# Joining the head of a vision-transformer kernel into one embedding loop, moving the zero stores to the sync engine, and reordering the first expert loads

## The chip, the cores and the metric

The kernel runs on one core of a Trainium2 chip. The metric is device time in microseconds (us), the median of three runs. The core has a matrix engine (PE, TensorE; its weight loads are listed as PEld), a vector engine (DVE), an activation engine (ACT), GpSimd (POOL), and a sync engine (SP), which here issues most of the DMAs. "SPq", "ACTq" and "PEq" in a profile are those engines' sequencers at work on register, wait and DMA-issue instructions.

## The reference

Input x is 32 images of 3 x 96 x 96. All values are float32.

```
h  = patches(x) @ W.T + b                      # 32 images x 36 tokens x 192
xm, ref = h[:22], h[22:]                       # 10 reference images
e(z) = gelu(z @ fc1 + b1) @ fc2 + b2           # 192 -> 48 -> 24, for own and reference tokens
mask = 0.5 + 0.5 * tanh(12.5 * mean over refs of cosine(e(xm), e(ref)))
k    = ref @ k_w ;  q, v = split(x @ qv_w)
three times, from x = xm * mask:
    a = q k^T * scale ; a = a a^T ; o = mean over refs of a v
    x = layernorm(o @ proj + b)
...                                            # combined with h, layernorm
x = x + softmax attention(layernorm(x))        # 12 heads, 36 tokens per image
x = x + mixture of 8 experts, top 2 (192 -> 768 -> 192)
out = layernorm(h + x)
```

Because `a a^T` only needs the product of the reference keys with themselves, the kernel forms one Gram matrix k^T k per pair of heads over all reference tokens and folds it into the query weights once.

## The kernel before

**Tiles.** The 1152 tokens are cut into NT = 11 tiles of T = 108 (three images); the last tile has 72. MT = 8 tiles hold tokens of the 22 own images; tile 7 holds own and reference images, and tiles 7 to 10 hold the references. The work is written out by hand per engine: each engine has a program of its own, and semaphores (`S["h_ready"]` and so on) order them. Nothing is scheduled by a planner.

**Head, in phases.** SP (L301 to L311) issues the loads: `tokw`, token tiles 0 and 1, the eleven small tensors of `EARLY`, token tiles 2 to 10, then `DIFF` and `FFN`. PE (L399 to L414) makes one token product per tile (L408, six matmuls of 192 columns, each recorded as two) into PSUM bank 0 or 1 and transposes the previous tile (L414). DVE adds the bias (L953), after a wait on all of `EARLY` (L950), and PE waits on the same set before tile 1 (L402). ACT copies each transpose to `hT` (L734). Then come, one after the other: the fc1 products in three chunks (L419), gelu (L737), four key products for tiles 7 to 10 (L425), eleven fc2 products (L429), the Gram matrices (L437), the folded weights `wqg` (L442), the sum of the reference embeddings `rb` (L449), and on DVE the squares and norms (L956 to L969), cosines (L973, L974), tanh on ACT (L754), the mask (L976 to L979) and the masked tiles `xs` (L981). The first transpose of the diffusion loop (L462) waits for `xs` of tile 0.

**Zeros.** The buffer `srt_dram`, into which the token rows are later scattered by expert, must hold zeros first. ACT issues nine stores for this (L740 to L742, 7.15 MB by the page's queue q10), placed between the gelus and the evictions of the key products (L743 to L750), so these evictions stand behind the nine issues in ACT's program.

**Middle.** Diffusion (NI = 24 turns of a software-pipelined loop, L468), then attention with the second layernorm, gate logits, top 2 and destination computation (L553). In both PE is the engine with the most work. In diffusion SP also stages the expert weights, ACT and POOL split them into two 16-bit parts.

**Experts.** POOL scatters the rows of each tile by two indirect DMAs (L1245). DVE computes which expert each of the NTILE = 25 tiles of 128 sorted rows belongs to (L1113 to L1130, `exp_ready`) and where its rows start (L1133, `place_ready`). SP waits for `exp_ready` (L359), issues the weights of the first WB = 3 tiles (L360, L349, two DMAs of 384 KB each), waits for `place_ready` and for all 22 scatters (L362, L363), and then loads the rows of the first tiles (L364, L356). PE transposes the rows of tile i+1 (L655) before the products of tile i. ACT, DVE and POOL scale and split the transposed rows, and PE does the expert's two layers (L669 to L671, L684 to L686). From the fourth tile on SP alternates rows and weights.

**End.** The results are scattered to `y_dram`, read back, summed and normalised.

## Time and profile before

| what | us |
|---|---|
| median of 3 runs (463.40 to 466.49) | 465.44 |
| the profiled execution's own time | 462.96 |
| its span, first to last instruction | 461.1 |
| first diffusion transpose starts | 65.36 |
| rows of the first expert tile arrive | 334.27 |

| engine | busy us | share of the span |
|---|---|---|
| PE | 370.7 | 80% |
| DVE | 249.3 | 54% |
| POOL | 213.8 | 46% |
| ACT | 202.5 | 44% |

How to read it: busy time is averaged over stages with different limits. The profiled execution took 1.9 us more than its span. The page's 40 slices (11.5 us each) show PE nearly full in most of them and nearly empty in the fifth (46 to 58 us), in those around 185 to 207 us, and around 320 to 334 us. The chain that ended last lists, from first to last instruction, the work or wait that each next step stood on; a piece on it has nothing beside it that ended later.

### The profile page before, as it was taken

How to read it: one execution, taken by the hardware profiler on the slowest of the kernel's cores; microseconds unless marked ns; L12 is line 12 of the kernel's file. 1: busy time of each engine (PE TensorE's matmuls, PEld its weight loads, DVE VectorE, ACT ScalarE, POOL GpSimd, SP SyncE). 2: the span in 40 equal slices, each digit the busy share in tenths (PEclk: the TensorE clock that was granted, in tenths of full speed). 3: DMA queues.
4: the chain of work that ended last, by engine and by line, in shares of the span. 5: the costliest groups of instructions: out<-in, count | busy, mean ns of one | idle time of the engine just before them, and what ended most of it. 6: DMA issues, size and time to landing. Idle time of an engine off the chain costs nothing.

```text
span 461.1 us, 10989 instructions
## 1 busy us (share of the span) xinstructions
PE 370.7 (80%) x3682; PEld 316.6 (69%) x3682; DVE 249.3 (54%) x713; ACT 202.5 (44%) x507; POOL 213.8 (46%) x355
## 2 busy tenths in 40 slices
PE   3998258999999974307999999974089999999964
PEld 3995245667667653206889999974079989999963
DVE  2111043445545476642467776756448888888723
ACT  1113313677777754213366567431054554444303
POOL 1000000276766655861256776545125666676424
PEclk9899559999999997555899999985569999999989
DMA  8905932665666653000000000013537767667042
GB/s 254 359 2 169 335 118 63 178 137 147 148 137 146 136 138 88 0 1 1 1 2 13 19 18 28 17 31 97 224 108 254 254 244 255 247 246 258 19 146 86
DMA packets 59558, 59.08 MB, mean 128 GB/s; under 512 B 36939, under 2 KB 46197, under 8 KB 58736
## 3 DMA queue, kind: packets, MB, share of 16 engines
q1 hardware_dynamic: 56240, 47.66, 34.2%
q10 hardware_dynamic: 1008, 7.15, 4.7%
q0 software_dynamic: 2256, 3.57, 2.5%
q8 instruction: 32, 0.52, 0.5%
q14 instruction: 22, 0.18, 0.1%
HBM read 25.11 MB, written 14.33 MB: 86 GB/s over the span
## 4 chain that ended last, share of the span: by engine, by line
PE 68%; DVE 8%; issue 7%; ACT 5%; POOL 4%; ACTq 3%; SPq 2%; DMA 2%; POOLq 0%; DVEq 0%
PE bank L385 37%; PE wide L385 26%; ACTq L741 3%; PE bank L390 3%; ACT xT L860 2%; DVE xs L1007 1%; PE bank L655 1%; POOL rstd L1212 1%; DMA bdm<-in_bdm 1%; SPq L349 1%; PE bank L569 1%; SPq L305 1%; ACT xTs L759 1%; DVE xT L1022 1%; ACT xs L777 1%
## 5 line engine op out<-in xcount | busy, mean ns | idle before, releaser
L1240 POOL TENSOR_TENSOR w1l<-xT,w1h 128x768 bf16<-128x768 f32 x8 | 13.2, 1644 | 81.1 <-ACT w1h L726 80.6
L1211 POOL TENSOR_SCALAR veps<-mv 108x1 f32<-108x1 f32 x46 | 11.0, 238 | 73.7 <-DVE mv L930 72.3
L1280 POOL DMA_INDIRECT y_dram<-ysb,ydst x25 | 25.9, 1038 | 36.4 <-DVE ydst L1165 28.1
L385 PE MATMUL wide<-w2h,xs 128*128 x300 | 39.1, 246 | 0.0
L385 PE MATMUL wide<-w2l,xs 128*128 x150 | 36.9, 246 | 0.0
L1159 DVE TENSOR_TENSOR xs<-xT,xs 128x384 bf16<-128x384 f32 x50 | 35.5, 711 | 1.7
L385 PE MATMUL bank<-wqv,xTs 128*108 128x384 f32 x96 | 35.9, 498 | 0.4 <-DVE xT L1022 0.4
L759 ACT ACTIVATE xT<-bank,gains 96x128 f32<-96x128 f32 x50 | 20.0, 449 | 36.8 <-PE bank L655 36.8
L385 PEld LDWEIGHTS bank<-xT 108*32 108x32 f32 (+4 forms) x332 | 15.7, 125 | 28.9 <-issue 17.0
L1157 DVE CAST xs<-xT 128x384 f16<-128x384 f32 x50 | 28.8, 577 | 11.6 <-ACT xT L895 11.5
L385 PE MATMUL bank<-xT 108*32 108x96 f32 (+4 forms) x332 | 22.7, 270 | 14.7 <-ACT xT L726 11.0
L385 PE MATMUL bank<-tokw,xT 128*108 128x192 f32 x132 | 26.5, 357 | 7.2 <-DMA xT<-in_xT 5.2
L385 PE MATMUL wide<-xT 64*108 64x36 f32 (+2 forms) x368 | 31.1, 279 | 0.9 <-ACT xT L726 0.9
L385 PE MATMUL bank<-wpa,ocT 128*108 128x192 f32 x96 | 24.4, 382 | 9.1 <-DVE yb L1019 6.3
L726 ACT ACTIVATE xT<-bank 108x192 f32<-108x192 f32 (+2 forms) x49 | 18.0, 372 | 30.1 <-PE bank L385 17.5
L385 PEld LDWEIGHTS wide<-xT 64*108 64x108 f32 (+1 forms) x368 | 29.0, 182 | 2.9 <-issue 2.4
L385 PE MATMUL bank<-xTs,wqk 128*128 128x108 f32 x176 | 28.0, 310 | 3.3 <-ACT xTs L759 3.3
L777 ACT ACTIVATE xs<-yb,shift,rstd 108x192 f32<-108x192 f32 x24 | 13.1, 547 | 36.7 <-POOL shift L1215 36.7
L1267 POOL TENSOR_TENSOR xl<-xT,xh 96x256 bf16<-96x256 f32 x25 | 21.4, 854 | 17.0 <-DVE xh L1147 16.3
L385 PEld LDWEIGHTS bank<-tokw,xT 128*108 128x108 f32 x132 | 23.5, 193 | 7.8 <-DMA tokw<-in_tokw 5.2
L1212 POOL TENSOR_TENSOR rstd<-veps,nhalf 108x1 f32<-108x1 f32 x46 | 26.3, 571 | 3.8
L385 PEld LDWEIGHTS bank<-xTs,wqk 128*128 128x128 f32 x176 | 24.6, 217 | 4.6 <-ACT xTs L759 3.3
(234 smaller groups left out, 1075.1 us busy)
## 6 DMA issues: line engine op xcount, KB each, us to landing
srt_dram<-row ACTq DMA_DIRECT2D x8, 800.2 KB, 10.2
xT<-in_xT SPq DMA_DIRECT2D x11, 324.0 KB
tokw<-w1h SPq DMA_DIRECT2D x9, 384.0 KB
e1T<-w1l SPq DMA_DIRECT2D x9, 384.0 KB
xT<-in_w SPq DMA_DIRECT2D x8, 384.0 KB, 3.5
hT<-in_w SPq DMA_DIRECT2D x8, 384.0 KB, 3.2
vecs<-w1h SPq DMA_DIRECT2D x8, 384.0 KB
wqv<-w1l SPq DMA_DIRECT2D x8, 384.0 KB
```

The source lines that it names most:

```text
L385: return nc.tensor.matmul(o, l, r, start=start, stop=stop)
L390: last = nc.tensor.transpose(o[:, f, :], i[:, f * HF:(f + 1) * HF], ident[0:T, 0:T])
L726: return nc.scalar.activation(o, i, ACT.Copy)
L741: nc.scalar.dma_start(srt_dram[z * 96:(z + n) * 96].rearrange("(p r) w -> p (r w)", p=96), blank[:, 0:n * W]).then_inc(S["zeroed"], 16)
L759: last = nc.scalar.activation(o[:, f], i[:, f], ACT.Identity, scale=gains[:, which, 0, f:f + 1], bias=gains[:, which, 1, f:f + 1])
L777: nc.scalar.activation(xs[:, p % MT], yb[:, p % 2], ACT.Identity, scale=rstd[0:T, n % 4:n % 4 + 1], bias=shift[:, n % 4:n % 4 + 1]).then_i ...
L1157: V.tensor_copy(high, hidf[:, i % 2, cols]).then_inc(S["hidh_ready"], 1)
L1159: V.tensor_tensor(hidl[:, i % 2, o].rearrange("p j n -> p (j n)"), hidf[:, i % 2, cols], high, ALU.subtract).then_inc(S["hidl_ready"], 1)
L1212: last = G.tensor_tensor(rstd[0:rows, k], ve, nhalf[0:rows], ALU.pow)
L1240: G.tensor_tensor(o, w, weights(q, 0)[0], ALU.subtract).then_inc(S["low_ready"], 1)
L1267: G.tensor_tensor(xl[0:HF, i % 2], x32[:, i % 2], xh[0:HF, i % 2], ALU.subtract).then_inc(S["xl_ready"], 1)
L1280: G.indirect_dma_start(y_dram, bass.IndirectOffsetOnAxis(ydst[:, q:q + 1], 0), ysb[:, q % YB], None, bounds_check=2 * NTOK - 1, oob_is_err ...
```

## The change

The head becomes one loop of NT + 3 = 14 steps over the tiles in the order 7, 8, 9, 10, 0, ..., 6 (`TILES`). Step s holds the token product of the s-th tile of that order, the fc1 product of tile s-2, the transpose of tile s-1, the fc2 product of tile s-3 and, for the four reference tiles, the key product of s-4. The Gram matrices and the reference sum stand in step 9, the folded weights in step 11. Token products use one PSUM bank (0), transposes one (1), fc1 one (4). The loads are reordered to match: `vecs` and `ident` (`FIRST`) behind the first tile, the nine others of `EARLY` behind the second. The nine zero stores are issued by SP behind all loads. The norms are made in two parts (references in steps 7 and 8, the rest behind the loop), by max and a power of -0.5 on POOL in place of ACT's square root and DVE's max and reciprocal; the own rows' norms are multiplied into the cosines instead of the embeddings. `kref` moves from the buffer of `xT` to tiles 7 to 10 of `xs`. A tanh on unused data stands behind ACT's loop. In the expert stage SP issues only the first tile's weights before its waits on places and scatters, then rows 0 and 1, weights 1, rows 2, weights 2.

```diff
@@ -34,7 +34,8 @@
 COS_EPS = 1e-8
 FIRST_REF = BM * N - (MT - 1) * T
 LAST = B * N - (NT - 1) * T
-CHUNKS = [(0, 4), (4, 4), (8, 3)]
+TILES = [*range(MT - 1, NT), *range(MT - 1)]
+NR = NT - MT + 1
 P = 128
 W = C + 2
 CAP = -(-B * N // P) * P
@@ -128,7 +129,7 @@
         qTb = spare[:, 1536:1968].rearrange("p (b u t) -> p b u t", b=2, u=2)
         osb = spare[0:T, 1968:1968 + OB * JB * C].rearrange("p (b j c) -> p b j c", b=OB, j=JB)
         oc = spare[0:T, 3696:4464].rearrange("p (b c) -> p b c", b=4)
-        kref = spare[0:T, 2832:3600].rearrange("p (b c) -> p b c", b=4)
+        kref = xs[:, MT - 1:]
         stage = [spare[:, 4464:4464 + HJ * C], spare[:, 4464 + HJ * C:4464 + 2 * HJ * C]]
         stage += [hT_all[:].rearrange("p k n -> p (k n)")[:, b * HJ * C:(b + 1) * HJ * C] for b in range(2)]
@@ -289,7 +291,8 @@
                 return (w1h, w1l)[low][:, e, k, :], stage[q % 4][:, 0:HID]
             return (w2h, w2l)[low][:, e].rearrange("p j c -> p (j c)"), stage[q % 4]
-        EARLY = ["vecs", "fc1", "fc1b", "fc2", "fc2b", "ident", "sel", "rowm", "kw", "wqT", "bdm"]
+        FIRST = ["vecs", "ident"]
+        EARLY = ["fc1", "fc1b", "fc2", "fc2b", "kw", "rowm", "sel", "bdm", "wqT"]
         DIFF = ["wq", "wqv", "pairm", "wpa", "gains"]
         FFN = ["wqk", "wvo", "amask", "gate", "route", "rank"]
         tiles = dict(gains=gains, vecs=vecs, fc1=fc1, fc1b=fc1b, fc2=fc2, fc2b=fc2b, ident=ident, sel=sel, rowm=rowm,
@@ -299,16 +302,23 @@
         @block.sync
         def _(sp):
             sp.dma_start(tokw[:], d["tokw"]).then_inc(tokw_in, 16)
-            for t in range(2):
...
-            for t in range(2, NT):
+            for s, t in enumerate(TILES):
+                if s == 1:
+                    for name in FIRST:
+                        sp.dma_start(tiles[name][:], d[name]).then_inc(first_in, 16)
+                if s == 2:
+                    for name in EARLY:
+                        sp.dma_start(tiles[name][:], d[name]).then_inc(early_in, 16)
                 sp.dma_start(xT[:, t], d["xT"][t]).then_inc(tile_in[t], 16)
             for name in DIFF:
                 sp.dma_start(tiles[name][:], d[name]).then_inc(attn_in, 16)
             for name in FFN:
                 sp.dma_start(tiles[name][:], d[name]).then_inc(ffn_in, 16)
+            sp.wait_ge(S["zeros_ready"], 1)
+            blank = row[0:96].rearrange("p t w -> p (t w)")
+            for z, n in ZEROS:
+                sp.dma_start(srt_dram[z * 96:(z + n) * 96].rearrange("(p r) w -> p (r w)", p=96),
+                             blank[:, 0:n * W]).then_inc(S["zeroed"], 16)
             sp.wait_ge(S["tok_psum"], NT)
             for i in range(NI + 1):
@@ -329,7 +339,7 @@
                     if (turn_of(q - 4) if q >= 4 else 0) != i:
                         continue
                     if q == 2:
-                        sp.wait_ge(S["e1_psum"], len(CHUNKS))
+                        sp.wait_ge(S["e1_psum"], NT)
                         sp.wait_ge(S["k_psum"], 4)
                     if q >= 4:
                         sp.wait_ge(S["low_ready"], q - 3)
@@ -357,12 +367,14 @@
             loaded = [None]
             sp.wait_ge(S["exp_ready"], 1)
-            for i in range(WB):
-                expert_weights(i)
+            expert_weights(0)
             sp.wait_ge(S["place_ready"], 1)
             sp.wait_ge(S["row_stored"], 16 * 2 * NT)
-            for i in range(WB):
-                sorted_rows(i)
+            sorted_rows(0)
+            sorted_rows(1)
+            expert_weights(1)
+            sorted_rows(2)
+            expert_weights(2)
             for i in range(WB, NTILE):
                 sorted_rows(i)
                 expert_weights(i)
@@ -397,58 +409,69 @@
             pe.wait_ge(tokw_in, 16)
-            for t in range(NT + 1):
-                if t == 1:
-                    pe.wait_ge(early_in, 16 * len(EARLY))
-                if t < NT:
+            for s in range(NT + 3):
+                if s < NT:
+                    t = TILES[s]
                     pe.wait_ge(tile_in[t], 16)
-                    if t >= 2:
-                        pe.wait_ge(S["h_ready"], t - 1)
+                    if s >= 1:
+                        pe.wait_ge(S["h_ready"], s)
                     for k in range(KF):
-                        last = mm(bank[t % 2][0:T, 0:C], xT[:, t, k, :], tokw[:, k, :], k == 0, k == KF - 1)
+                        last = mm(bank[0][0:T, 0:C], xT[:, t, k, :], tokw[:, k, :], k == 0, k == KF - 1)
                     last.then_inc(S["tok_psum"], 1)
-                if t >= 1:
...
-            last.then_inc(S["rb_psum"], 1)
+                if 0 <= s - 2 < NT:
+                    t = TILES[s - 2]
+                    if s == 2:
+                        pe.wait_ge(early_in, 16 * len(EARLY))
+                    pe.wait_ge(S["hT_ready"], s - 1)
+                    if s >= 3:
+                        pe.wait_ge(S["e1_ready"], s - 2)
+                    for k in range(2):
+                        last = mm(bank[4][0:E1, 0:T], fc1[:, k, :], hT[:, k, t * T:(t + 1) * T], k == 0, k == 1)
+                    last.then_inc(S["e1_psum"], 1)
+                if 0 <= s - 1 < NT:
+                    if s == 1:
+                        pe.wait_ge(first_in, 16 * len(FIRST))
+                    pe.wait_ge(S["h_ready"], s)
+                    if s >= 2:
+                        pe.wait_ge(S["hT_ready"], s - 1)
+                    turn(halves(1), h[:, TILES[s - 1]]).then_inc(S["hT_psum"], 1)
+                if 0 <= s - 3 < NT:
+                    t = TILES[s - 3]
+                    pe.wait_ge(S["e1_ready"], s - 2)
+                    place = bank[5][0:T, (t - MT + 1) * E2:(t - MT + 2) * E2] if s - 3 < NR else bank[7][0:T, t * E2:(t + 1) * E2]
+                    last = mm(place, e1T[:, t * T:(t + 1) * T], fc2[:])
+                    if s - 3 == NR - 1:
+                        last.then_inc(S["exr_psum"], 1)
+                    if s - 3 == NT - 1:
+                        last.then_inc(S["ex_psum"], 1)
+                if 0 <= s - 4 < NR:
+                    i = s - 4
+                    if i >= 2:
+                        pe.wait_ge(S["k_ready"], i - 1)
+                    for k in range(2):
+                        last = mm(bank[2 + i % 2][0:T, 0:C], hT[:, k, TILES[i] * T:(TILES[i] + 1) * T], kw[:, k, :], k == 0, k == 1)
+                    last.then_inc(S["k_psum"], 1)
+                if s == 9:
+                    pe.wait_ge(S["k_ready"], NR)
+                    for f in range(2):
+                        for i in range(NR):
+                            rows = T if i < NR - 1 else LAST
+                            a = kref[0:rows, i, f * HF:(f + 1) * HF]
+                            last = mm(bank[6][0:HF, f * HF:(f + 1) * HF], a, a, i == 0, i == NR - 1)
+                    last.then_inc(S["g_psum"], 1)
+                    pe.wait_ge(S["exn_ready"], 1)
+                    for i in range(NR):
+                        rows = T if i < NR - 1 else LAST
+                        last = mm(bank[5][0:T, 128:128 + E2], sel[0:rows, int(i > 0), :], ex[0:rows, MT - 1 + i, :], i == 0, i == NR - 1)
+                    last.then_inc(S["rb_psum"], 1)
+                if s == 11:
+                    pe.wait_ge(S["g_ready"], 1)
+                    for k in range(2):
+                        for f in range(2):
+                            last = mm(bank[3][0:HF, k * C + f * HF:k * C + (f + 1) * HF],
+                                      wqT[:, f, k * HF:(k + 1) * HF], gbd[:, f, :])
+                    last.then_inc(S["wqg_psum"], 1)
             def to_features(i):
                 if i < MT:
@@ -729,27 +752,20 @@
                 return bank[b][0:HF, 0:2 * T].rearrange("p (f t) -> p f t", f=2)
             halves2 = bank[0][0:HF, 2 * T:4 * T].rearrange("p (f t) -> p f t", f=2)
-            for t in range(NT):
...
-            nc.scalar.activation(nrm[:], nrm[:], ACT.Sqrt).then_inc(S["nrm_ready"], 1)
+            for s in range(NT + 3):
+                if 0 <= s - 2 < NT:
+                    t = TILES[s - 2]
+                    act.wait_ge(S["e1_psum"], s - 1)
+                    nc.scalar.activation(e1T[:, t * T:(t + 1) * T], bank[4][0:E1, 0:T], ACT.Gelu, bias=fc1b[:, 0:1]).then_inc(S["e1_ready"], 1)
+                if 0 <= s - 1 < NT:
+                    t = TILES[s - 1]
+                    act.wait_ge(S["hT_psum"], s)
+                    copy(hT[:, :, t * T:(t + 1) * T], halves(1)).then_inc(S["hT_ready"], 1)
+                if 0 <= s - 4 < NR:
+                    i = s - 4
+                    act.wait_ge(S["k_psum"], i + 1)
+                    nc.scalar.activation(kref[:, i, :], bank[2 + i % 2][0:T, 0:C], ACT.Copy, scale=rowm[:, 3:4] if i == 0 else 1.0).then_inc(S["k_ready"], 1)
+            nc.scalar.activation(mask[:, 0:1], rowm[:, 0:1], ACT.Tanh)
             act.wait_ge(S["cos_ready"], 1)
             nc.scalar.activation(th[:], cosm[:], ACT.Tanh, scale=12.5).then_inc(S["th_ready"], 1)
@@ -947,31 +963,41 @@
             link(V.memset(ones8[:], 1.0))
             link(V.memset(ends[:, 0:1], 0.0))
             link(V.memset(ydst[:], 1 << 20))
-            dve.wait_ge(early_in, 16 * len(EARLY))
...
-                            bdm[:, 1:2, :].broadcast_to([HF, 2, HF]), ALU.mult).then_inc(S["g_ready"], 1)
+            dve.wait_ge(first_in, 16 * len(FIRST))
+            for s, t in enumerate(TILES):
+                dve.wait_ge(S["tok_psum"], s + 1)
+                V.tensor_tensor(h[:, t], bank[0][0:T, 0:C], vec(V_TOKB), ALU.add).then_inc(S["h_ready"], 1)
+                refs = slice(MT - 1, NT)
+                if s == 7:
+                    dve.wait_ge(S["exr_psum"], 1)
+                    dve.wait_ge(early_in, 16 * len(EARLY))
+                    link(V.tensor_tensor(ex[:, refs], bank[5][0:T, 0:NR * E2].rearrange("p (t e) -> p t e", t=NR),
+                                         fc2b[:, None, :].broadcast_to([T, NR, E2]), ALU.add))
+                    link(V.tensor_tensor(exs[:, refs], ex[:, refs], ex[:, refs], ALU.mult))
+                    V.tensor_reduce(nrm[:, refs], exs[:, refs], AX_X, ALU.add).then_inc(S["sq_ready"], 1)
+                if s == 8:
+                    dve.wait_ge(S["nrm_ready"], 1)
+                    V.tensor_tensor(ex[:, refs], ex[:, refs], nrm[:, refs, None].broadcast_to([T, NR, E2]), ALU.mult).then_inc(S["exn_ready"], 1)
+                if s == 10:
+                    dve.wait_ge(S["g_psum"], 1)
+                    V.tensor_tensor(gbd[:], bank[6][0:HF, 0:C].rearrange("p (f c) -> p f c", f=2),
+                                    bdm[:, 1:2, :].broadcast_to([HF, 2, HF]), ALU.mult).then_inc(S["g_ready"], 1)
+                    dve.wait_ge(S["rb_psum"], 1)
+                    link(V.tensor_copy(rb[:], bank[5][0:T, 128:128 + E2]))
             dve.wait_ge(S["wqg_psum"], 1)
             dve.wait_ge(attn_in, 16 * len(DIFF))
             V.tensor_copy(wqv[0:HF, :, 0:C], bank[3][0:HF, 0:2 * C].rearrange("p (k c) -> p k c", k=2)).then_inc(S["wqg_ready"], 1)
-            dve.wait_ge(S["nrm_ready"], 1)
...
-            link(V.tensor_copy(rb[:], bank[6][0:T, 0:E2]))
+            own_t = MT - 1
+            dve.wait_ge(S["ex_psum"], 1)
+            link(V.tensor_tensor(ex[:, 0:own_t], bank[7][0:T, 0:own_t * E2].rearrange("p (t e) -> p t e", t=own_t),
+                                 fc2b[:, None, :].broadcast_to([T, own_t, E2]), ALU.add))
+            link(V.tensor_tensor(exs[:, 0:own_t], ex[:, 0:own_t], ex[:, 0:own_t], ALU.mult))
+            V.tensor_reduce(nrm[:, 0:own_t], exs[:, 0:own_t], AX_X, ALU.add).then_inc(S["sq_ready"], 1)
+            dve.wait_ge(S["sq_ready"], 2)
             link(V.tensor_tensor(exs[:, 0:MT], ex[:, 0:MT], rb[:, None, :].broadcast_to([T, MT, E2]), ALU.mult))
-            V.tensor_reduce(cosm[:], exs[:, 0:MT], AX_X, ALU.add).then_inc(S["cos_ready"], 1)
+            link(V.tensor_reduce(cosm[:], exs[:, 0:MT], AX_X, ALU.add))
+            dve.wait_ge(S["nrm_ready"], 2)
+            V.tensor_tensor(cosm[:, 0:own_t], cosm[:, 0:own_t], nrm[:, 0:own_t], ALU.mult).then_inc(S["cos_ready"], 1)
             dve.wait_ge(S["th_ready"], 1)
             link(V.tensor_scalar(mask[:], th[:], 0.5, 0.5, ALU.mult, ALU.add))
@@ -1228,6 +1254,10 @@
             G.memset(row[:], 0.0).then_inc(S["zeros_ready"], 1)
             link(G.memset(nhalf[:], -0.5))
+            for n, span in enumerate((slice(MT - 1, NT), slice(0, MT - 1))):
+                pool.wait_ge(S["sq_ready"], n + 1)
+                link(G.tensor_scalar(nrm[:, span], nrm[:, span], COS_EPS ** 2, None, ALU.max))
+                G.tensor_tensor(nrm[:, span], nrm[:, span], nhalf[0:T].broadcast_to([T, span.stop - span.start]), ALU.pow).then_inc(S["nrm_ready"], 1)
             for i in range(3, NI + 6):
                 if 5 <= i < NI + 5:
                     root(offset=True)
```

## Rows read from the trace of the kernel before

**Rows 1.** Chain that ended last, head: start us, us, engine, tile and line.
```profile
6.48 4.48 DMA bdm<-in_bdm
...
17.20 1.95 PE bank L385 x12
19.16 0.19 PE bank L390 x2
...
34.97 4.13 PE wide L385 x12
...
53.97 0.42 ACT xT L748
...
55.11 2.89 PE bank L385 x16
...
58.43 1.61 PE bank L385 x8
...
61.47 1.65 PE wide L385 x8
...
64.99 1.48 DVE xs L981 x6
```

**Rows 2.** Timeline of the head: start us, us, engine, line, operation, idle before it.
```profile
5.20 3.77 PE L385 MATMUL bank<-tokw,xT 128*108 128x192 f32 x12 [5.20 <-DMA xT<-in_xT]
...
11.00 3.38 PE L385 MATMUL bank<-tokw,xT 128*108 128x192 f32 x12 [2.03 <-DMA bdm<-in_bdm]
11.04 0.36 DVE L953 TENSOR_TENSOR h<-bank,vecs 108x192 f32<-108x192 f32 x1 [7.26 <-DMA bdm<-in_bdm]
...
16.80 0.40 SPq L311 DMA_DIRECT2D rank<-in_rank  x1
...
35.37 1.28 ACT L737 ACT_TABLE_LOAD   x1
...
39.02 2.85 PE L385 MATMUL bank<-kw,hT 96*108 96x192 f32 x16
39.13 0.53 ACT L737 ACTIVATE e1T<-wide,fc1b 48x324 f32<-48x324 f32 x1 [0.47 <-PE wide L385]
39.13 14.79 ACTq L741 DMA_DIRECT2D srt_dram<-row  x9
41.80 2.27 PE L385 MATMUL wide<-fc,e1T 48*108 48x24 f32 x22
...
65.36 0.59 PE L390 MATMUL bank<-ident,xs 108*96 108x108 f32 x2 [2.26 <-DVE xs L981]
```

**Rows 3.** Two windows of the head: busy us by engine, granted clock, DMA share, GB/s.
```profile
44.00:55.00 11.00, 0.07 (x1) 0.00 (x0) 1.29 (x3) 1.03 (x4) 0.00 (x0) 0.59 1.00 336
55.00:58.00 3.00, 2.87 (x16) 2.63 (x16) 0.00 (x0) 2.83 (x4) 0.00 (x0) 0.50 0.94 315
```

**Rows 4.** The power on POOL at the kernel's end: minimum, median, maximum ns.
```profile
L1286 POOL TENSOR_TENSOR rsa<-rsa,nhalf x4: 733/883/891, 447.2 to 455.5; 108x3 f32<-108x3 f32 x3, 108x2 f32<-108x2 f32 x1
```

**Rows 5.** SyncE's DMA issues at the start of the expert stage.
```profile
325.62 0.58 SPq L349 DMA_DIRECT2D tokw<-w1h  x1
326.33 0.52 SPq L349 DMA_DIRECT2D e1T<-w1l  x1
...
332.16 3.70 SPq L356 DMA_DIRECT2D xT<-srt_dram  x4
```

**Rows 6.** Chain that ended last, start of the expert stage.
```profile
330.39 0.02 SPq L363
...
332.16 2.10 DMA xT<-srt_dram
...
341.12 0.43 PE bank L655 x2
```

**Rows 7.** The scatters of the attention stage's end: last issue and time to landing.
```profile
L1245 POOL DMA_INDIRECT srt_dram<-row,dst x9: 989/990/1110, 300.3 to 323.6; - x9
...
DMA to landing us min/median/max: 2.5/2.6/3.8
```

More of the change, by code:

```diff
@@ L237, in vit_kernel @@
         S = {}
-        for name in ("tok_psum h_ready hT_psum hT_ready e1_psum e1_ready ex_psum sq_ready nrm_ready "
+        for name in ("tok_psum h_ready hT_psum hT_ready e1_psum e1_ready exr_psum ex_psum sq_ready nrm_ready "
                      "exn_ready rb_psum cos_ready th_ready k_psum k_ready g_psum g_ready wqg_psum wqg_ready "
@@ L427, in _ @@
-            pe.wait_ge(S["e1_ready"], len(CHUNKS))
-            for t in range(NT):
-                last = mm(bank[7][0:T, t * E2:(t + 1) * E2], e1T[:, t * T:(t + 1) * T], fc2[:])
-            last.then_inc(S["ex_psum"], 1)
-            pe.wait_ge(S["k_ready"], 4)
-            for f in range(2):
-                for i in range(4):
-                    rows = T if i < 3 else LAST
-                    a = kref[0:rows, i, f * HF:(f + 1) * HF]
-                    last = mm(bank[2][0:HF, f * HF:(f + 1) * HF], a, a, i == 0, i == 3)
```

63 lines of the change are left out of this document (1 added, 62 removed).

## The prediction

> **What bounds the kernel now.** I read the chain that ended last first, because the change touches two stretches where PE is not full and only the chain tells whether their waits count. In the head [rows 1] the token loop runs on PE without a gap (tile product 1.95, transpose 0.19, so 2.14 a tile), the fc1 chunks take 4.13, and then the chain leaves PE: ACT's first key eviction starts at 53.97. The timeline [rows 2] tells why. ACT's sequencer is on the nine zero stores from 39.13 for 14.79 us; the key products had started at 39.02 and the fc2 products, started at 41.80, ended at about 44.1. From there the Gram matrices, folded weights and the reference sum each wait for the one before, PE runs at the lower of its two levels (granted clock 0.50, 1.2 GHz, in 55 to 58, after 11 us with 0.07 us of matmul [rows 3]), and diffusion begins at 65.36. Before that, PE and DVE also stood from 8.97 to 11.00 for the last small load, landed at 10.96 [rows 1, 2]. At the expert stage SP issues the first weight DMAs at 325.62, reaches the wait for the scatters at 330.39, and issues the first rows at 332.16, landed 2.10 later [rows 5, 6]. PE does nothing for the output in that time. So both edits lie on the path.
>
> **The new head, PE.** All its work at the upper level (2.4 GHz), worked out per kind: 11 token products at 1.95 = 21.45 and 11 transposes at 0.19 = 2.09 [rows 1]; fc1 has the same columns in eleven pieces instead of three, 4.13 [rows 1]; keys 2.85 and fc2 2.27 [rows 2]; the Gram matrices, folded weights and reference sum were measured at the lower level, 2.89, 1.61 and 1.65 [rows 1], and stand now inside a full loop, so half: 1.45, 0.80, 0.83. Sum 35.87. On top:
> - The first tile starts as before at 5.20 and takes 3.77, 1.82 over 1.95 [rows 2].
> - The second tile took 3.38 at 11.00, when PE had stood for 2 us; now it starts about 0.4 behind the first. Its excess lies between 0 and 1.43; I take the middle, 0.75.
> - With one PSUM bank, tile s+1 waits for the bias add (0.36 [rows 2]). The first time nothing stands between, 0.40; the second time only a transpose, 0.20. Later an fc1 product (4.13/11 = 0.38) and a transpose cover it. Without that cover it would be 0.4 x 11 = 4.4 in all.
> - In the last steps fc1 of tile s waits for a copy behind the transpose, 0.2, and the last fc2 product for the last gelu. That gelu has a quarter of a chunk's columns; under 0.53 [rows 2], less the fc2 product of the tile before: 0.2.
>
> PE's end of the head: 5.20 + 35.87 + 1.82 + 0.75 + 0.60 + 0.40 = 44.64.
>
> **Behind it, DVE, POOL and ACT.** Three DVE operations on 7 tiles x 24 numbers, each at most 0.36 as the add of 192 columns [rows 2], with hand-overs 1.1. Then POOL's max and power: the power took 733 ns for 2 columns and 883 for 3 [rows 4], so 0.15 a column and about 1.5 for 7; with the max and hand-overs (my allowance) 1.8. DVE's two cosine operations (0.75) lie beside it. Last come a multiply (0.2), tanh and three mask operations (0.8, small DVE operations at some 0.2) and the first masked tile, 1.48/6 = 0.25 [rows 1]. Start of diffusion 44.64 + 1.1 + 1.8 + 1.3 = 48.9. The unknown here is POOL: with a power of 0.57 as for one column, which the median of 883 speaks against, 0.9 less; if the column cost grows to 0.3, 1.1 more. I add 0.6 for changes of work on PE; the loop's rows show none (17.20 + 1.95 = 19.15, next at 19.16 [rows 1]), 0.1 for each of its some 45 groups would be 4.5. That gives 49.5: **15.9 us less** than 65.36.
>
> **Edits costed at nothing.** *Zeros on SP.* SP's last load issue ends at 17.20 [rows 2]; its next work is the first scratch store of diffusion, before at about 76 and now near 60. Even at ACT's pace (14.79) the issues end near 32. In the queue the stores stand behind every load, so no token tile waits for them. If they did run into the scratch stores, each turn's round trip would be late. *Load order.* FIRST and the second tile are requested earlier than the last of EARLY was; landed by 9.4 they are covered by the first tile, and each microsecond later costs one. The third tile is the 15th request in both orders. *Table load.* Gelu's load, 1.28 [rows 2], stands in the loop behind the first copy; the second tile's product (1.95 or more) covers it. *Early norm work in steps 7 and 8, gbd and rb in step 10.* Each hides behind a step of some 2.7 us of PE. *Folded weights to wqv.* Behind the last fc1 product and gelu.
>
> The page "ScalarE: Activation LUTs" of the Trainium skill (What ACT_TABLE_LOAD costs) counts 2.66 us for a switch because of a drain behind the load. By that figure this load would stick out by 0.7 at most, once.
>
> **The start of diffusion.** Before, its first matmuls were at 1.2 GHz. Now PE pauses for about 4.3 us instead of standing at the lower level since 46. Half of the first two turns' matmul work, about 1.5, is the most that can be gained, nothing the least. In 44 to 55 the mean of 0.59 means that the clock fell about 2 us after work ended [rows 3], so it will mostly be low again: 0.3.
>
> **The expert stage.** The first two weight DMAs are issued by 326.33 + 0.52 = 326.85 [rows 5]. The last scatter starts at 323.6; scatters land 2.5 to 3.8 after issue [rows 7], so at 326.1 to 327.4. Taking 327.1 for 330.39, the rows come 3.3 sooner, at 331.0 instead of 334.27. Bounds: if the 3.8 counts from the end of the last 0.99 us issue, 328.4 and a gain of 2.0; with no wait for scatters 3.5. Next late would be rows 1, which PE transposes before tile 0's products; they follow rows 0 at once, as before (3.70 for four [rows 5]). Weights 1 are issued from about 330.5, weights 2 from 333; four row loads and six weight DMAs fit before the second tile, which began at 341.12 [rows 6] and now needs its weights near 338. Cover some 3 us. **3.3 us less.**
>
> Sum: 15.9 + 0.3 + 3.3 = 19.5. Against the profiled execution: 462.96 - 19.5 = 443.5. The three runs' median is 465.44, which gives 445.9; between them I forecast 444.5.
>
> **Rivals.**
> 1. *Only part is gained: each change of work on PE or each wait costs 0.1* (and POOL's power is at its dear end). Head gains 15.9 - 3.9 - 1.1 = 10.9, total 14.5, time 450. For it: eleven rounds of four short kinds of work; against: no gap between products and transposes now [rows 1]. Chance 0.10.
> 2. *Issuing elsewhere saves little.* As a mechanism of this kernel: the 7.15 MB still go out, at 336 GB/s in 44 to 55 [rows 3], some 21 us, and work that needs DMA pays them later. If only nine plain issues at the 0.40 of rows 2 are saved, 3.6 of 14.8, the forecast loses 11: 455.5. Against: PE waits for no transfer between 17 and 60 us except token tiles ahead of the zeros; the 14.79 are issue time with ACT's evictions behind. Chance 0.05. The Trainium skill's page "DMA: Bandwidth & Descriptors" (Issuing engines are not separate DMA queues) states that another issuing engine saves only the sequencer's issue time, usually small beside the DMA. By that rule the edit is worth little; the row says that here the issue is as long as the transfer.
> 3. *Slower: the loop stays at 1.2 GHz.* Place: steps 2 to 13. If bank and copy waits leave PE so broken up that the clock does not rise, its remaining 34 us of work take 68. Diffusion would start near 83, some 18 later than before; less 3.3, and from the middle of 462.96 and 465.44, the time is 479. It decides once over half of the loop (17 of 34 us) runs low. For it: tile 2's 3.38 and the 0.50 after the pause in 44 to 55 [rows 2, 3]. Against: the same kind of work ran at the upper rate with small pauses. Chance 0.03.
> 4. *The row edit does nothing* because the scatters end late or the rows queue behind weights 0: 448. Chance 0.08.
>
> **How the numbers follow.** The forecast's case has 0.74: 440.5 (cheap POOL, warm start, rows 3.5) to 447. With rivals 1 and 4, and half of the spread of the runs, the range is 440.5 to 450.5 and holds about 0.85 of the chance. A measurement of this kernel can tell about 1% (4.7 us) from no change. All cases but 3 and a remainder are faster by that: faster 0.93, same 0.03, slower 0.04.
>
> **What would show it.** ACT issues no DMA; the first key eviction comes near 25 us; PE is full from 12 to 41; diffusion's first transpose lies at 49 to 50; the nine stores on SP end before 40; SP's first row load is issued near 329 and PE's first row transpose is near 331. The forecast is wrong if PE waits in the loop for `hT` or `h` in most steps, if the POOL power takes over 2.5 us, or if first(1) waits for its weights.

## The result, and the profile after

The changed kernel takes 452.24 us (median of 6 runs, 449.3 to 453.15), the kernel before, run beside it, 465.03 (462.9 to 466.49): ratio 0.9723, 95% interval 0.9689 to 0.9757. It is faster, by 12.8 us, where 20.9 were forecast, and 452.24 lies above the range. The profiled run of the changed kernel is its fastest, 449.3 (span 447.5). Against the profiled 462.96 of before the gain is 13.7, where the sum said 19.5.

The chain that ended last, in the changed kernel's head (start us, us, engine and tile), answers to [rows 1]:

```profile
21.52 2.78 PE bank L397 x16
24.30 0.50 PE wide L397 x4
24.80 0.32 PE bank L402 x2
...
25.42 2.78 PE bank L397 x16
...
45.16 0.34 ACT e1T L759
...
45.87 0.57 PE wide L397 x4
...
50.40 0.42 POOL nrm L1259
50.89 1.53 POOL nrm L1260
53.56 1.48 DVE xs L1007 x6
```

Look for a loop in which PE hardly waits and which is still too slow: the step from 21.52 to 25.42 is 3.90 long. The products of a tile and of a key take 2.78 of it where the sum had 2.66, fc1 takes 0.50 where it had 0.38, the transpose 0.32 where [rows 1] had 0.19, and fc2 (25.12 to 25.42 in the same chain) 0.29 where it had 0.21. PE leaves the loop at 49.22, not at 44.64.

From the timeline of the same stretch, for [rows 2]:

```profile
5.06 3.69 PE L397 MATMUL bank<-tokw,xT 128*108 128x192 f32 x12 [5.06 <-DMA xT<-in_xT]
9.39 2.17 PE L397 MATMUL bank<-tokw,xT 128*108 128x192 f32 x12 [0.65 <-DMA xT<-in_xT]
16.88 4.87 SPq L320 DMA_DIRECT2D srt_dram<-row  x9
22.39 0.42 ACT L767 ACTIVATE xs<-bank,rowm 108x192 f32<-108x192 f32 x1 [0.78 <-PE bank L397]
53.94 0.60 PE L402 MATMUL bank<-ident,xs 108*96 108x108 f32 x2 [4.73 <-DVE xs L1007]
```

The zeros are issued in 4.87 us on SP, the first key is evicted at 22.39 instead of 53.97, and diffusion begins at 53.94: 11.4 us less than 65.36, where 15.9 were forecast.

Two windows (busy us of PE, weight load, DVE, ACT, POOL, then granted clock, DMA share, GB/s), for [rows 3]:

```profile
12.00:41.00 29.00, 28.82 (x182) 24.39 (x183) 3.70 (x12) 8.15 (x22) 1.28 (x2) 1.00 1.01 367
55.00:59.00 4.00, 3.94 (x14) 2.94 (x15) 0.86 (x4) 0.69 (x2) 0.00 (x0) 0.50 0.00 0
```

The loop ran at the upper level (granted clock 1.00, 2.4 GHz), diffusion's start at the lower as before.

SP's issues and the chain at the expert stage, for [rows 5] and [rows 6]:

```profile
316.67 0.58 SPq L359 DMA_DIRECT2D tokw<-w1h  x1
...
319.17 1.90 SPq L366 DMA_DIRECT2D xT<-srt_dram  x2
```

```profile
319.17 2.00 DMA xT<-srt_dram
```

The first rows are issued 2.50 us after the first weights; in the kernel before it was 6.54. One thing stands in the attention's first tile that the prediction did not have:

```profile
206.37 1.28 ACT L886 ACT_TABLE_LOAD   x1
207.66 0.56 ACT L886 ACTIVATE xT<-xT 108x432 f32<-108x432 f32 x1
```

### The profile page after: what moved, and what is told of

Its sections match the earlier page's. It is cut to its first block, busy times and chain, and to the rows that moved or that the text cites. A ratio compares the mean times of both kernels' runs of the same rounds, so it can differ in the third digit from the quotient of the medians.

```text
span 447.5 us, 11080 instructions
## 1 busy us (share of the span) xinstructions
PE 370.0 (83%) x3714; PEld 314.5 (70%) x3714; DVE 248.0 (55%) x715; ACT 202.9 (45%) x514; POOL 217.2 (49%) x359
## 4 chain that ended last, share of the span: by engine, by line
PE 73%; DVE 7%; issue 6%; ACT 5%; POOL 4%; DMA 3%; SPq 2%; POOLq 0%; ACTq 0%; DVEq 0%
PE bank L397 38%; PE wide L397 29%; PE bank L402 3%; ACT xT L876 2%; DVE xs L1033 1%; PE bank L678 1%; DMA xT<-in_xT 1%; POOL rstd L1238 1%; PE bank L592 1%; SPq L311 1%; ACT xTs L775 1%; DVE xT L1048 1%; ACT xs L793 1%; ACT ocT L749 1%; POOL shift L1241 1%
## 5 line engine op out<-in xcount | busy, mean ns | idle before, releaser
L397 PE MATMUL bank<-tokw,xT 128*108 128x192 f32 x132 | 25.2, 344 | 6.1 <-DMA xT<-in_xT 6.1
L397 PEld LDWEIGHTS bank<-tokw,xT 128*108 128x108 f32 x132 | 22.4, 183 | 6.9 <-DMA tokw<-in_tokw 5.0
L1275 POOL DMA_INDIRECT srt_dram<-row,dst x22 | 23.1, 1049 | 7.6 <-issue 6.0
L397 PEld LDWEIGHTS wide<-w2h,xs 128*128 128x128 f16 (+1 forms) x300 | 26.4, 98 | 0.0
L397 PEld LDWEIGHTS bank<-xT 108*32 108x32 f32 (+2 forms) x316 | 13.3, 118 | 17.3 <-issue 16.9
```

The costliest lines, as they stand in the source:

```text
L397: return nc.tensor.matmul(o, l, r, start=start, stop=stop)
L1275: G.indirect_dma_start(srt_dram, bass.IndirectOffsetOnAxis(dst[:, t, k:k + 1], 0), row[:, t, 0:W], None, bounds_check=EXP * CAP - 1, oob_i ...
```

## The experiments

Most are one edit of the changed kernel, or of the kernel before where it says so; 4 and 9 combine several. A letter names a theory throughout.

**1. Wider arrays: is it the change of work on PE?** fc1 uses 48 columns of the array and fc2 reads 48 rows. Padded with zeros to 96, their streamed columns stay the same.

```
-  fc1 = sb("fc1", [HF, 2, E1])
+  fc1 = sb("fc1", [HF, 2, HF])
-  mm(bank[4][0:E1, 0:T], fc1[:, k, :], ...)
+  mm(bank[4][0:HF, 0:T], fc1[:, k, :], ...)
```

> The changed kernel with the fc1 weights padded by zeros from 48 to 96 columns, so that this product fills as many columns of the array as a transpose; the fc2 product stays 48 rows deep. In the changed kernel's loop a step costs 0.50 us of fc1, 0.32 of transposes and 0.29 of fc2, where 0.38, 0.19 and 0.21 were summed from the phases of before. Theory A (each change between products of a different part of the array exposes the next weight load, about 0.1 us): fc1 falls to about 0.38 and the transposes behind it to 0.19, 2.5 us less over eleven steps, the first diffusion transpose at 51.5 instead of 53.94. Theory B (the semaphore waits in front of each piece cost this time): nothing moves by more than 0.3 us.

The second kernel also widens `fc1b`, `fc2` and `e1T`, and the gelu runs on 96 partitions:

> The changed kernel with fc1 padded to 96 columns and fc2 to 96 rows of weights (zeros; the gelu runs over 96 rows). Theory A: fc1 0.38, transposes 0.19, fc2 0.21, together 0.33 less in each of eleven steps, diffusion starts near 50.3 and the kernel takes about 3.6 us (0.8%) less than the changed one, some 448.6 against 452.2, ratio to before 0.965. Theory B: the same step times as now, diffusion at 53.9, ratio 0.972.

Measured: 451.05 (one run) and 447.71 (4 runs, 447.22 to 448.54; ratio 0.9625, 0.9573 to 0.9676). The chain of the first and then of the second, one step each:

```profile
26.22 0.37 PE wide L397 x4
26.59 0.19 PE bank L402 x2
...
29.86 0.37 PE wide L397 x4
```

```profile
24.55 0.37 PE wide L397 x4
...
25.11 0.12 PE wide L397 x2
25.23 2.67 PE bank L397 x16
27.90 0.37 PE wide L397 x4
```

Twice the columns of the array, and fc1 and the transpose behind it are 0.13 shorter each; with fc2 wide too, fc2 is 0.17 and what follows it 0.11 shorter. The steps are 3.64 (26.22 to 29.86) and 3.35 (24.55 to 27.90) for 3.90, and the transpose at 24.92 takes 0.19 in the second too. Theory A holds: the sum's own step (1.95 + 0.38 + 0.19 + 0.21 + 0.71 = 3.44) is met once the width no longer changes. In both profiles diffusion still began at 54.1, because they started worse: the first two tiles took 4.14 or 4.15 each, and in the second kernel the first tile came only at 7.47. The repeats of 7 have the same two slow tiles and begin diffusion at 56.4, so like for like the first kernel gains 2.3 there and the second, with its start 2.3 later, some 4.6.

The timeline also shows what is exposed. First the transpose behind fc1 in the changed kernel, then in the first wide one (PEld is the weight load):

```profile
24.73 0.12 PEld L402 LDWEIGHTS bank<-ident,h 108*96 108x96 f32 x1 [0.15 <-DVE h L969]
24.73 0.30 PE L402 MATMUL bank<-ident,h 108*96 108x108 f32 x1
```

```profile
26.34 0.22 PEld L402 LDWEIGHTS bank<-ident,h 108*96 108x96 f32 x2
26.43 0.26 PE L402 MATMUL bank<-ident,h 108*96 108x108 f32 x1
```

With fc1 wide the transpose's weights start 0.09 ahead of its product, beside the last fc1 product. Behind the 48-column fc1 they start only with it. (The bracket names a semaphore; experiment 2 takes that wait away, and load and product still start together, at 29.24.)

**2. Fewer semaphore waits.** The transpose's and fc2's waits that an earlier wait of the step already covers were left out.

```
-  pe.wait_ge(S["h_ready"], s)
-  if s >= 2: pe.wait_ge(S["hT_ready"], s - 1)
+  if s < 2 or s >= NT: pe.wait_ge(S["h_ready"], s)
   turn(halves(1), h[:, TILES[s - 1]])
```

> The changed kernel without the waits of PE's loop that an earlier wait of the same step already implies (in front of the transposes the waits for h and hT, in front of fc2 the wait for e1). Theory B: transposes fall from 0.32 to about 0.19 and fc2 from 0.29 to 0.21, 2.2 us less, diffusion near 51.7. Theory A: no step changes, diffusion at 53.9 within 0.2.

One run took 448.23. fc1 and the transpose are what they were, so theory B falls:

```profile
28.81 0.50 PE wide L397 x4
29.31 0.32 PE bank L402 x2
```

The lower time is no effect of the waits: diffusion began at 54.54, later than in the first profile. The attention's first tile (from its mask, DVE, to its first output) took 17.54 where the changed kernel took 19.47; the granted clock was 0.93 in 201 to 203 where the changed kernel had 0.50.

**3. The kernel before with only the zeros moved to SP**: ACT's block of nine stores stands behind SP's load issues instead, all else is before's.

> The kernel before with one edit: the nine zero stores go out on SyncE behind the loads; head in phases, expert loads as before. Theory C (the head's gain is the zeros off ACT's queue, the joined loop adds nothing): key evictions run near 40 to 42, the Gram matrices start behind fc2 at 44.1 and at the upper clock, then 1.5 + 0.4 + 0.8 and the norm and cosine chain of before; diffusion's first transpose near 51.3, 14 us before the 65.36 of before and 2.6 before the changed kernel's 53.94; ratio to before 0.970. Theory D (the joined loop carries a good part of the gain): diffusion not before 56, ratio 0.98 or more.

452.13 (4 runs, 451.44 to 454.52), ratio 0.9735 (0.9675 to 0.9796): one moved block gives the time of the whole change (452.24). One line of ACT's timeline, and one of the chain:

```profile
41.19 0.42 ACT L748 ACTIVATE xT<-bank,rowm 108x192 f32<-108x192 f32 x1 [0.31 <-PE bank L390]
```

```profile
45.30 1.54 PE bank L390 x16
```

The first key eviction follows the last gelu, 40.36 to 40.89, at once (41.19, before 53.97), the Gram products run at the upper clock (1.54 for 2.89 in [rows 1]), and diffusion starts at 54.21. The joined loop starts it at 53.94.

**4. All four combinations.** The kernel before with both other edits (SP's zeros, early rows) but its own head; and the changed kernel with its zeros back on ACT's queue, between the loop and the tanh.

> The kernel before with two of the change's edits, the zeros sent by SP and the rows issued behind the first expert's weights, but with its own head: no joined embedding loop, chunks of four tiles, the square root on ScalarE. Theory I (joining the loop is worth nothing beside these two): 452.1 of the kernel before with SP's zeros alone, less 4.1, is 448, so faster than the whole change by some 4 (the changed kernel also pays 1.3 for its table load in the attention). Rival J (the joined loop carries a gain of its own, of 2 us or more, that the trace of the zeros' run hid behind a lucky start): 452 or more.

> The changed kernel with the nine stores of zeros back on ScalarE's queue, behind its part of the joined loop and ahead of the table load and the tanh of the cosines. With it the four combinations of loop and queue are there. Theory C (the queue of the zeros is the head's gain, not the loop): ScalarE is busy issuing from 46 to about 59 or 61, the tanh waits for it, the first diffusion transpose starts at 62 to 66 (53.9 in the changed kernel, 65.4 before), and the time is about 458 to 461. Rival D (the joined loop alone brings a good part of the gain): diffusion starts by 58, time 455 or less. Rival K, on the attention's tiles, whose period was 8.40 before and 8.5 to 9.0 in all five runs with SP's zeros: if the zeros' queue is what lengthens them, they are back at 8.40 here.

The first: 448.35 (4 runs, 447.57 to 448.57), ratio 0.9625 (0.9592 to 0.9658), which lies wholly below the 0.9689 to 0.9757 of the whole change. Theory I holds, J falls: the joined loop, with the table load that came with it, costs 3.9 us by the medians. In the profiles it is 1.9 at the start of diffusion (54.48, against 56.4 in the repeats of 7) and some 1.3 in the attention's first tile (18.03, against 19.1 to 19.6). The second: 465.23 (one run), no better than before, though it has the early rows. Its ACT:

```profile
51.01 14.88 ACTq L766 DMA_DIRECT2D srt_dram<-row  x9
65.93 0.20 ACT L768 ACTIVATE mask<-rowm 108x1 f32<-108x1 f32 x1 [14.59 <-issue]
```

Diffusion starts at 67.25, later than forecast since the issues took their full 14.88 from a loop end at 51. Theory C holds and D falls. K falls as well: the attention's tiles were long here too, up to 9.03.

**5. Is it ScalarE's queue, or the moment?** The same block as ACT's first work, ahead of the loop.

> The changed kernel with the nine stores of zeros on ScalarE's queue as its first work, ahead of the loop (ScalarE has nothing else until 10.9). Theory T (what costs 15 us on ScalarE's queue is that the queue fills and each further issue waits for the transfers, whichever engine issues them): the issues take 12 us or more here too, from 2.6 to 15 or later, the first eviction and with it the loop start 4 us or more late, and the inputs, which share the 16 engines with the zeros, land later: 455 or more. Rival U (on an engine that issues early, the nine issues take 5 us as on SP): no more than 1 slower than the changed kernel, 453 or less.

474.33 (one run). ACT's and PE's timeline:

```profile
2.65 12.53 ACTq L753 DMA_DIRECT2D srt_dram<-row  x9
20.28 0.35 ACT L744 ACTIVATE hT<-bank 96x216 f32<-96x216 f32 x1 [3.78 <-PE bank L397]
```

```profile
16.14 3.92 PE L392 MATMUL bank<-tokw,xT 128*108 128x192 f32 x12 [6.61 <-DMA xT<-in_xT]
33.36 3.85 PE L392 MATMUL bank<-tokw,xT 128*108 128x192 f32 x12 [13.12 <-DMA xT<-in_xT]
```

Issuing takes 12.53 there as well, so rival U falls: the moment does not set it. Theory T's other half, "whichever engine issues them", does not hold for SP alone, which issued the same nine in 4.87. But in this run SP's own issues grew long too while ACT's zeros went out: those of the small inputs took 1.10 to 2.02 each from 4.16 to 16.5 (0.34 to 0.43 in the changed kernel), and the nine tile loads 14.08 for 4.62. So long issues are not ACT's alone. Why nine zero stores issued by SP stay short, no trace shows. The 7.15 MB sent beside the inputs hold the second tile back to 16.14 and the third to 33.36.

**6. The rows and the table.** SP's old order in the changed kernel (`for i in range(WB): expert_weights(i)`, the wait, `for i in range(WB): sorted_rows(i)`):

> The changed kernel with SP's order at the expert stage as before: the weights of all three first experts, then the wait for the scatters, then the rows of all three. Theory G (the new order gains what the path shows, 4.1 us from the packing of the counts to the first expert's cast): slower than the changed kernel by 3.5 to 4.5, median about 456. Rival H (what the early rows gain is lost again behind, as the second and third expert's weights land later): slower by under 2, below 454.

456.22 (4 runs, 453.34 to 457.48), ratio 0.9808 (0.9771 to 0.9845) against 0.9723: the edit is worth 4.0 us by the medians, as theory G has it (452.13 against 448.35 of 3 and 4 say 3.8). Its SP:

```profile
317.25 0.58 SPq L359 DMA_DIRECT2D tokw<-w1h  x1
...
323.55 1.78 SPq L366 DMA_DIRECT2D xT<-srt_dram  x2
```

And the dummy activation behind the loop as an exponential:

```
-  nc.scalar.activation(mask[:, 0:1], rowm[:, 0:1], ACT.Tanh)
+  nc.scalar.activation(mask[:, 0:1], rowm[:, 0:1], ACT.Exp)
```

> The changed kernel with one thing altered: the one-element activation that loads ScalarE's table behind the embedding loop uses the exponential instead of the hyperbolic tangent. Theory E (the change took the square root off ScalarE, and with it the loading of a table that holds both tanh and exp, so that the attention's first exponential must load one at 206.4 in the path, 1.28 us): the load near 206 is gone, one stands in the head behind the last gelu, before the cosines are there, so hidden; the span falls by 1.0 to 1.3, to a median of about 451.0 where the changed kernel has 452.2. Rival F (the exponential's table has no tanh, so that the load moves to the cosines, which are in the path too): no gain, or up to 1.3 slower, 452.2 to 453.5.

```profile
49.05 1.28 ACT L768 ACT_TABLE_LOAD   x1
...
52.95 0.21 ACT L770 ACTIVATE th<-cosm 108x8 f32<-108x8 f32 x1 [2.40 <-DVE cosm L1000]
```

The tanh at 52.95 needs no load of its own, and none is left near 206. Theory E's mechanism is shown, and F falls. The Trainium skill, "ScalarE: Activation LUTs" (Table sets), lists tanh with exp; the trace agrees. The time, 451.19 (449.89 to 454.48; ratio 0.9714, 0.9662 to 0.9767), cannot be told from 452.24. The load stood on the chain with all of its 1.28. From the attention's start to its first output this kernel took 18.67 us, where the changed kernel took 19.47 (19.55 and 19.14 in the repeats of 7), so 0.8 came back in this pair of profiles: the matmuls behind ran some 0.6 longer here, more of them at the lower clock. The same stretch took 17.5 to 20.6 in other kernels that have the load, so a few profiles do not fix its price.

**7. Where the rest of the median is: repeats.** The changed kernel twice more, and the kernel before once more, each for a profile.

> The changed kernel once more, for a second profile. Its profiled run of 449.3 was the fastest of six with a median of 452.24; the prediction missed by 5.8 us against the profiled run and by 7.7 against the median, and these 2 to 3 us are in no trace so far. Theory R (the other runs have a later rise of the clock in the head, two products at the low clock instead of one, some 2 to 4 us before the first diffusion step): a run of 451 or more shows its first diffusion transpose at 56 or later. Rival S (the loss sits in the attention's tiles or the stretch of low clock behind the diffusion): the transpose at 54 and attention or diffusion longer by 2.

> The same kernel as the run before, for a third profile, with the same two theories: a time above 451 goes with a first diffusion transpose at 56 or later by theory R, and with a longer diffusion or attention by rival S.

> The kernel before once more, for a second profile. Theory P (the attention's tiles of 8.5 to 9.0, seen from the fourth on in all eight kernels profiled since, come with the changes): the period is 8.40 throughout, as in the first profile of before. Rival Q (they differ between executions of the same kernel, and the first profile of before had none of the long ones): some tiles of 8.5 to 9.0 here too, attention some 1 to 1.5 longer.

The changed kernel took 453.63 and 452.23. PE in the first of them:

```profile
5.16 4.14 PE L397 MATMUL bank<-tokw,xT 128*108 128x192 f32 x12 [5.16 <-DMA xT<-in_xT]
9.95 4.14 PE L397 MATMUL bank<-tokw,xT 128*108 128x192 f32 x12 [0.65 <-DVE h L969]
14.64 2.17 PE L397 MATMUL bank<-tokw,xT 128*108 128x192 f32 x12 [0.18 <-DVE h L969]
56.37 0.59 PE L402 MATMUL bank<-ident,xs 108*96 108x108 f32 x2 [4.73 <-DVE xs L1007]
```

Both repeats have the second tile at the lower clock (4.14 for 2.17) and diffusion at 56.37 and 56.42, 2.4 later than in the first profile: theory R holds. (The record of the granted clock begins with its first rise, and the views print 1.00 before it; there the length of the products tells the level.) S does not hold for the attention (115.6 and 115.9 us in the repeats, 116.1 in the first profile), but 453.63 has another 2.1 us behind the packing of the counts, which neither theory named. The chain puts them at the kernel's end, where the results are read back. First the changed kernel's first profile, then this one:

```profile
428.25 2.37 DMA xT<-y_dram
```

```profile
431.33 3.65 DMA xT<-y_dram
```

From the landing of the last result to PE's next product it is 2.52 us in the one and 4.52 in the other.

The kernel before took 465.97. The attention's outputs (DVE) in before's first profile and in its repeat:

```profile
253.53 0.36 DVE L1106 TENSOR_TENSOR yb<-wide,xs 108x192 f32<-108x192 f32 x1 [0.69 <-PE wide L385]
261.93 0.36 DVE L1106 TENSOR_TENSOR yb<-wide,xs 108x192 f32<-108x192 f32 x1 [1.39 <-PE wide L385]
```

```profile
255.32 0.36 DVE L1106 TENSOR_TENSOR yb<-wide,xs 108x192 f32<-108x192 f32 x1 [0.68 <-PE wide L385]
264.61 0.36 DVE L1106 TENSOR_TENSOR yb<-wide,xs 108x192 f32<-108x192 f32 x1 [2.28 <-PE wide L385]
```

The period is 8.40 in the one and 9.29 in the other: rival Q holds. The first profile of before had an attention 2.7 us shorter (114.2 us from its start to the packing of the counts, 116.9 in the repeat, 116.1 in the changed kernel), and the change has no part in it.

**8. Three products of zeros on PE ahead of the first tile**, to have the clock up sooner (`gbd` cleared by DVE first, results never read):

> The changed kernel with three products of a zeroed 96 by 192 tile (3.7 us at the low clock) ahead of the first tile, while TensorE waits for its first transfers (until 5.06); nothing reads what they make. Theory N (where the clock rises in the head differs from one execution to the next, 8.1 to 16.7 in the profiles, and the joined loop, in which TensorE hardly idles, pays for it: this is why the changed kernel's runs spread over 449.3 to 453.15): the clock rises by 8 in every run, the runs lie within 1.5 us of each other, median 448.5 to 450. Rival O (the spread has another cause): median 451 to 453 and a spread of 3 or more, as without them.

454.37 (6 runs, 451.28 to 457.03), ratio 0.9749 (0.9702 to 0.9796) against 0.9723: not faster, and spread wider than without. In its profile the three took 2.23 us (1.12 to 3.35), not the 3.7 expected, and PE then stood until the first tile at 5.34; the clock was up at 9.9 and only one tile ran at the lower level. So a late clock costs what 7 shows, but these products do not cure it in the median, and theory N falls as the one reason for the spread.

**9. The changed kernel with its losses mended.** Both products wide; the exponential's table; own norms of five tiles and then of two; in the last steps transpose and eviction ahead of fc1 and gelu:

```
-  if s - 3 == NT - 1:
+  if s - 3 in (8, NT - 1):
       last.then_inc(S["ex_psum"], 1)
...
+  own_norms(0, 5, 1)
   dve.wait_ge(S["wqg_psum"], 1)
...
+  own_norms(5, own_t, 2)
```

> The changed kernel with five edits, all results the same: both small products widened to 96 columns of the array (the padding is zeros), the exponential's table loaded behind the loop, the own tiles' norms in two lots (five tiles while the loop's last steps run, then two), and in the loop's last steps the turn and its eviction ahead of the first small product and its gelu. Estimate from the profiles: 447.7 of the kernel with both products wide, less 0.8 for the table, 0.9 for the power of 2 columns where there were 7, 0.5 for the order at the end: 445.5, range 444.5 to 448. Rival: the norms' second lot adds three small VectorE operations in the path, which eat what the power gives back: 447.

> The five edits of the run before last together with the three products ahead of the first tile. Theory N: 1 to 2 less than with the five edits alone, about 444. Rival O: the same as those within 0.5.

445.08 (6 runs, 442.73 to 447.16), ratio 0.9531 (0.9487 to 0.9575), as estimated, and with the three products 445.0 (442.23 to 445.92), ratio 0.9539: no difference, once more against N. This beats the changed kernel and the 448.35 of experiment 4. Its chain at the loop's end:

```profile
46.04 0.38 PE bank L397 x2
...
47.23 0.40 POOL nrm L1272
...
47.70 0.73 POOL nrm L1273
```

The power takes 0.73 for two columns, 1.53 for seven; diffusion starts at 49.94, though this run's first tile came only at 6.44.

## Why the prediction was wrong, by its own steps

- **The head, PE: failed, and it is the miss.** The prediction priced each kind of work by rows in which it ran in long batches ([rows 1, 2]) and added no more than 0.6 for the changes of work, since "the loop's rows show none". They could not: before's loop alternates two kinds with nearly the same part of the array (108 and 96 columns). In the joined loop the 48-column fc1 and the 48-row fc2 stand between them: fc1 0.12, transpose 0.13, fc2 0.08 and key with tile 0.12 over the sum, 0.45 a step. Over eleven steps (keys in four) that is some 4.1 of the 4.6 by which PE left late; the two tile products that stand right behind an fc2, with no key between, took 2.13 for 1.95 each and add 0.4. Experiment 1 shows the cause, the change of the array's part, and in its rows the weight load that no longer runs ahead; why the load waits at such a change is not shown. Rival 1 had this mechanism at 0.1 a change, with a chance of 0.10 and a time of 450. Its half on changes is what happened. Its half on waits fell in experiment 2, and POOL's power was not at its dear end (1.53).
- **End of the loop: right.** fc1 of the last tile but one waits for a copy behind a gelu, and starts at 45.87. PE does the transpose and fc2 until 45.73 and so stands for only 0.14, where 0.2 was forecast.
- **Behind the loop: right.** From PE's end to diffusion it took 4.72, forecast 4.2; the allowance of 0.6 was for PE. POOL's max and power took 0.42 and 1.53, in sum 1.95 for 1.8.
- **Second tile: wrong in the typical run.** It was given 0.75 for the middle between no excess and 1.43. The first profile had 0.2, the two repeats 2.2, above the bound of 1.43, as the clock had not risen. The kernel before is indifferent to it: its head began diffusion at 65.36 and 65.31 with the clock up at 8.4 (and down again for a while) and at 14.1, for the zeros' issues set the end there. A full PE loop has no such cover.
- **Zeros on SP: right, and more than that.** It was the whole gain of the head (experiments 3 and 4), which the prediction left undivided between loop and queue. Rival 2 falls, since nothing paid for the transfers later. The Trainium skill's page "DMA: Bandwidth & Descriptors" (Issuing engines are not separate DMA queues) says that another issuer saves only the sequencer's issue time, which is usually small beside the DMA. The first half agrees: that time was the gain. The second does not hold here: nine issues held ACT's sequencer for 14.79, 14.88 and 12.53 us. In before's chain each behind the first took 1.72 to 2.14, where its 800 KB at the 336 GB/s of [rows 3] take an estimated 2.4, and the measurement decides.
- **Table load: missed.** The prediction looked at gelu's load only. With the square root gone, ACT goes from gelu straight to tanh, and nothing loads the table that the attention's exponential needs, until 206.37. It is on the chain with 1.28, and 0.8 came back in experiment 6. The exponential starts 0.01 behind the load: of the 2.66 with a drain that the Trainium skill's page "ScalarE: Activation LUTs" (What ACT_TABLE_LOAD costs) gives, this trace shows the load alone.
- **Start of diffusion:** 0.3 forecast, nothing came. The granted clock was 0.50 as before. From the first transpose to the attention it took 145.3 us, in the two profiles of before 144.8 and 146.2.
- **Rows: right in mechanism, a little more.** From the packing of the counts to the first expert's cast it took 7.54 for 11.67, 4.1 less, where 3.3 were forecast. The scatters had landed when SP asked, the cheap end of the bound (3.5), and from the last weight issue ahead of the rows to the first row issue it took 0.55 less. Weights 1 and 2 were in time. Rival 4 falls by experiment 6.
- **Rival 3** (the loop at 1.2 GHz) did not occur: 1.00 in 12 to 41.
- **The anchor.** The sum was set against a profile of before with a short attention, and the forecast placed between it and the median. Typical against typical, the sum gives 465.03 - 19.5 = 445.5, and 452.24 is 6.7 above it; the other 1.0 of the 7.7 is the anchor's. By stages: head 65.3 to 56.4 = 8.9 where 15.9 were forecast (7.0 short), table some 0.8, diffusion's start 0.3, rows 0.8 better, in sum 7.3, which is 0.6 too much and within what the profiles differ by.

**Open:** why the runs of the changed kernel and of experiments 6, 8 and 9 spread over 3.7 to 5.8 us, when those of experiment 4's first kernel and of the wide one lie within 1.3. The later clock explains 2.4 us between the three profiles of the changed kernel, not experiment 8. Also open are the 2.0 us at the read back, which the profile of experiment 9's first kernel shows too (3.76 for 2.37), and what lengthens the attention's tiles from the fourth on.

## What to carry to other kernels

When a change interleaves small products of different shapes, price them by rows in which such neighbours alternate, not by batches; if none exist, give the rival with a price per change more than a remote chance (here it had 0.10), and look in the timeline whether the next weight load still starts ahead of its product. Padding to the neighbour's width is a cheap edit to try (452.24 to 447.71 here). Split a change into its edits before crediting the large one: here a block of nine issues moved to another queue was the gain, and the loop built around it cost 3.9 us; with its widths mended alone (447.71) it is level with the kernel that keeps the old loop (448.35). When an activation function leaves an engine, follow the table loads down to the next function that needs one, and take a second profile of the kernel before: an anchor can be off by 2.7 us in a stage that the change does not touch.

## What the runs showed of the hardware that was not expected

- A 48-column product between 96- and 108-column ones costs 0.13 us itself and 0.13 at its neighbour; a 48-row one 0.17 and 0.11. Padded to 96, both are gone. At such a change the weight load starts with its product (24.73), not 0.09 ahead (26.34 and 26.43).
- Nine stores of up to 800 KB take ACT 12.5 to 14.9 us to issue, SP 4.6 to 4.9. While ACT's went out, SP's small issues took up to 2.02 each.
- The first tiles' clock rose at 8.1 in one execution and at 14.3 and 14.4 in two others of the same kernel, with the first product at 5.06 to 5.21 in all of them.
- Three products of zeros ahead of the first tile changed no median for the better (454.37 against 452.24; 445.0 against 445.08).
